# A decoder layer on one core: cross-attention queries projected per tile of 125 rows, low halves moved to GpSimd, and a rearranged prologue

## The reference, cut to what matters

```
x = x + attn(layernorm(x))               # causal, 16 query heads, 4 key/value heads of 128,
                                         # layernorm and rotary embedding of q and k
x = x + cross(layernorm(x), context)     # 32 heads of 16; q, k, v = x Wq.T, ctx Wk.T, ctx Wv.T
                                         # q = q * rsqrt(mean(q*q) + eps) per head, k the same
                                         # softmax(q k.T / 4) v, no output projection
x = x + ffn(layernorm(x))                # 2048 wide, silu(x Wu.T) * (x Wg.T) Wd.T,
                                         # weights rounded to -s, 0, +s with s = mean |W|
```

## Time and profile before

| what | value |
|---|---|
| three executions, median | 1393.27 us |
| the profiled execution's own time | 1391.79 us |
| its span | 1389.7 us |
| TensorE matmul, busy | 1314.8 us (95%) |
| VectorE, busy | 784.6 us (56%) |
| ScalarE, busy | 640.9 us (46%) |
| GpSimd, busy | 274.8 us (20%) |
| mean granted clock of TensorE | 0.984 of full speed |
| chain that ended last | 84% TensorE, 6% VectorE, 3% issue, 1% ScalarE |

### The profile page before, as it was taken

One profiled execution on the slowest core, in us unless ns is written; L12 is line 12 of the kernel. 1 busy time (PEld: TensorE's weight loads), 2 busy tenths in 40 slices (PEclk: granted clock), 3 DMA queues, 4 the chain that ended last, 5 costly groups with the idle time before them and its releaser, 6 DMA issues.

```text
span 1389.7 us, 27539 instructions
## 1 busy us (share of the span) xinstructions
PE 1314.8 (95%) x10968; PEld 867.6 (62%) x10968; DVE 784.6 (56%) x1942; ACT 640.9 (46%) x1452; POOL 274.8 (20%) x266
## 2 busy tenths in 40 slices
PE   7689999999999999999999999999999779999996
PEld 6456666666666666566666666666666446565543
DVE  6987776777677775434445434444346784444422
ACT  3243354333333355366666666666667223232321
POOL 0244452434244441111111111111111000000000
PEclk9799999999999999999999999999999999999999
DMA  8400000000000003111111111112203410000000
GB/s 267 161 1 1 1 1 1 1 1 1 1 1 1 1 1 124 47 58 63 46 46 46 46 45 46 45 47 68 66 25 139 159 68 23 0 24 1 23 1 28
DMA packets 23604, 59.99 MB, mean 43 GB/s; under 512 B 1214, under 2 KB 10811, under 8 KB 20405
## 3 DMA queue, kind: packets, MB, share of 16 engines
q1 hardware_dynamic: 23477, 58.24, 12.6%
HBM read 54.96 MB, written 3.28 MB: 42 GB/s over the span
## 4 chain that ended last, share of the span: by engine, by line
PE 84%; DVE 6%; issue 3%; ACT 1%; DVEq 0%; ACTq 0%
PE A L1616 21%; PE A L1529 11%; PE C L1940 10%; PE A L1583 10%; PE C L1640 6%; PE B L1657 5%; PE C L1569 3%; PE C L1554 3%; PE A L1956 2%; PE B L1956 2%; PE A L1538 2%; PE B L1625 2%; PE B L1562 2%; PE B L1546 2%; DVE qk L1120 1%
## 5 line engine op out<-in xcount | busy, mean ns | idle before, releaser
L1616 PE MATMUL A<-wxhl,arena 128*122 128x512 f16 x1152 | 265.3, 380 | 0.0
L1616 PEld LDWEIGHTS A<-wxhl,arena 128*122 128x122 f16 x1152 | 149.1, 134 | 88.0 <-issue 8.3
L1940 PE MATMUL C<-arena 128*128 128x375 f16 (+1 forms) x1024 | 188.2, 337 | 5.1 <-DVE arena L1121 5.1
L1529 PE MATMUL A<-arena,wxhl 128*125 128x512 f16 (+1 forms) x780 | 174.9, 382 | 6.1 <-DVE tub L960 4.3
L1940 PEld LDWEIGHTS C<-arena 128*128 128x128 bf16 x1024 | 100.4, 98 | 82.7 <-issue 9.6
L506 POOL TENSOR_TENSOR arena<-arena,region 100x512 f32<-100x512 f32 (+1 forms) x64 | 65.9, 1062 | 421.2 <-DVE region L1084 421.2
L690 ACT ACTIVATE arena<-C 122x1600 f32<-122x1600 f32 x96 | 144.3, 1503 | 4.4 <-PE C L1640 2.8
L1529 PEld LDWEIGHTS A<-arena,wxhl 128*125 128x125 f16 (+1 forms) x780 | 105.0, 137 | 65.7 <-DVE tub L960 4.8
L482 POOL TENSOR_TENSOR region<-tub 125x512 f32<-125x512 f32 (+1 forms) x65 | 82.6, 1270 | 265.4 <-DVE tub L960 265.3
L618 ACT ACTIVATE region<-C,negm 100x100 f32<-100x100 f32 x256 | 84.3, 358 | 102.2 <-DVE negm L1004 102.2
L1583 PE MATMUL A<-arena,stageb 128*125 128x512 f16 (+1 forms) x416 | 123.8, 379 | 0.7 <-ACT arena L674 0.7
(11 more groups left out here) (163 smaller groups left out, 2096.5 us busy)
## 6 DMA issues: line engine op xcount, KB each, us to landing
stageb<-in_wffn SPq DMA_DIRECT2D x16, 768.0 KB, 4.7
arena<-in_ctxt SPq DMA_DIRECT2D x16, 722.0 KB, 4.7
stageb<-in_wffn SPq DMA_DIRECT2D x6, 1024.0 KB, 4.8
wxhl<-in_wffn SPq DMA_DIRECT2D x6, 1024.0 KB, 4.8
arena<-in_wqkv SPq DMA_DIRECT2D x4, 1024.0 KB, 15.4
arena<-in_wx SPq DMA_DIRECT2D x3, 1024.0 KB, 6.9
out_x<-xres SPq DMA_DIRECT2D x12, 250.0 KB
xres<-in_x SPq DMA_DIRECT2D x1, 2250.0 KB
```

The source lines that it names most:

```text
L1529: ins = pe.matmul(A[j % 2][0:m, :], xp[:, k, at:at + m], wp[:, j, k, :], start=(n == 0), stop=(n == 11))
L1616: ins = pe.matmul(A[(par + n) % 2][0:rows, :], lhs, wp[:, 0 if n == 0 else 1 if n < 4 else 2, k, :], start=(i == 0), stop=(i == 11))
L1940: ins = pe.matmul(C[2 * (e % 2) + half][:, 0:cols], wf[:, 3 * (e // 4) + half, k, (e % 4) * 128:(e % 4 + 1) * 128], part[:, k, 0:cols], st ...
```

## The change

It has five parts.

1. **Queries per tile.** `project_q(i)` projects the queries of tile i (125 rows), 13 times, in place of 16 `project2(b, 0)`; it is issued at the end of `turn(b)` if `x2_tile(b)` is a tile, which it isn't in turns 2, 7, 12, 14 and 15. `turn_queries(i)` turns all four blocks of the tile at once into B[0], and VectorE's `queries_back(i)` writes them with their parity copies into one of two buffers `qms`. `turn_heads` and `keys_back` only handle keys. At the end of a turn, TensorE's order is now `scores2(b, 5)`, `turn_queries`, `project2(b + 1, 6)`, a wait for `queries_back`, `turn_heads(b + 1, 0)`, `attend2(b, 2)`, `scores2(b + 1, 0)`, and the rest as before.
2. **Low halves of unit 0 on GpSimd.** In unit 0 of the feed-forward part the 16 `hidden_lo` are GpSimd's.
3. **Filler matmuls.** 14 float32 matmuls of 128 columns ahead of the first `centre`, and 14 behind `values_of(0)`.
4. **Output weights.** The low halves of matrices 5, 6, 8 and 7 are made by GpSimd (2048 elements per partition each), after ScalarE has scaled the float32 source in place (`w_scaled`). The waits on them move with them. `w_lo(9)` stays on VectorE and moves from behind the second to behind the fourth group of turn 0. The rotary tables of tiles 1 to 3 are made in the loop of tile 0, not after it.
5. **Head sums.** For tile 0, groups 1 and 3 are scaled by ScalarE (`z_part`, 4 instructions each), not by GpSimd.

The diff, cut to its core:

```
+WARM, FILL = 14, 14
+def q_tile(b):
+    return last_tile(b) if b == 0 or last_tile(b) > last_tile(b - 1) else None
...
 # GpSimd
-            for j in range(5):
+            def w_lo(j, nth):
+                dst, hi = (wql[:, j], wqh[:, j]) if j < 6 else (wohl[:, W_GROUP[j], 1], wohl[:, W_GROUP[j], 0])
+                pool.wait_ge(a_ws, nth)
+                pool.tensor_tensor(dst..., staged(j)[0]..., hi..., ALU.subtract).then_inc(g_wlo, 1)
+            for j in range(3):
                 w_of(0, j)
-            for j in range(5):
-                z_of(0, j)
+            w_lo(5, 1)
+            for j in range(3, 5):
+                w_of(0, j)
+            for j in (0, 2, 4):
+                z_of(0, j, 2 if j else 1)
+            w_lo(6, 2)
+            w_lo(8, 3)
+            w_lo(7, 4)
...
+            n = unit_cols(0)
+            for e in range(ET):
+                pool.wait_ge(*count("a_hh", 0, e + 1))
+                if e >= 2:
+                    pool.wait_ge(*count("pe_dn", 0, e - 1))
+                pool.tensor_tensor(hl[e % 2][:, 0:n], hd[e % 2][:, 0:n], hh[e % 2][:, 0:n], ALU.subtract)\
+                    .then_inc(g_hl, 1)
...
 # ScalarE
                 elif 8 <= j < 10:
-                    act.wait_ge(d_wlo, {8: 1, 9: 4}[j])
+                    act.wait_ge(g_wlo, {8: 1, 9: 3}[j])
...
+            def w_scaled(j):
+                act.activation(staged(j)[0], staged(j)[0], ACT.Copy, scale=SW).then_inc(a_ws, 1)
...
-                if j == 2:
+                if j == 1:
                     w_hi(5)
+                elif j == 2:
+                    w_scaled(5)
+                elif j == 3:
+                    w_hi(6)
+                elif j == 4:
+                    w_scaled(6)
             v_of(0)
+            w_hi(8)
+            z_part(1)
+            z_part(3)
             x_hi(1, A[1])
-            for j in range(6, 10):
-                w_hi(j)
+            w_scaled(8)
+            w_hi(7)
+            w_scaled(7)
+            w_hi(9)
...
                 exp2(b, 5)
+                if end < 2:
+                    values(b + 1, 2, odd)
+                    keys_back(b + 1, 0)
                 out_back(b, 2)
-                if end < 2:
-                    keys_back(b + 1, 0)
-                    values(b + 1, 2, odd)
...
 # VectorE
+            def queries_back(i):
+                n = rows_of(i)
+                dve.wait_ge(*count("pe_qT", i, 1))
+                for b, lo, hi, at in pieces(i):
+                    if b > 1:
+                        dve.wait_ge(*count("pe_sc", b - 2, NU))
+                    q = B[0][:, 0:NT * n]...[:, :, at:at + hi - lo].unsqueeze(2).broadcast_to([128, NT, 2, hi - lo])
+                    ins = dve.tensor_tensor(qms[b % 2][:, :, :, lo:hi], q, parity, ALU.mult)
...
-            dve.wait_ge(ld_g, 32)
-            tables(slice(0, 1))
-            dve.wait_ge(d_tab, 4)
             for j in range(5):
                 if j < 4:
                     for half in range(2):
                         w_centred_lo(j + 1, half)
+                if j == 0:
+                    dve.wait_ge(ld_g, 32)
+                    tables(slice(0, 1), ((0, 2), (1, 0)))
+                    dve.wait_ge(d_tab, 4)
                 proj(0, j)
                 if j == 1:
                     columns()
-                if j == 2:
-                    w_lo(5)
+                elif j == 2:
+                    dve.wait_ge(ld_r, 16)
+                    tables(slice(1, 4), ((0, 2),))
                 elif j == 3:
+                    tables(slice(1, 4), ((1, 0),))
                     dve.wait_ge(ld_x1, 16)
                     row_stats(1, ssq[:, 20:21])
             head_norm(0)
             normed(1, rstd[:, 20:21])
-            dve.wait_ge(ld_r, 16)
-            tables(slice(1, 4))
             dve.wait_ge(d_tab, 10)
-            z_back(0, 0, B[0])
+            for j in range(5):
+                z_back(0, j, B[j % 2])
             x_lo(1, A[1])
-            z_back(0, 1, B[1])
-            w_lo(6)
-            z_back(0, 2, B[0])
-            z_back(0, 3, B[1])
-            w_lo(7)
-            z_back(0, 4, B[0])
...
-                if b == 0:
-                    w_lo(8)
...
-                    if b == 0 and g == 1:
+                    if b == 0 and g == 3:
                         w_lo(9)
...
 # TensorE
+            def project_q(i, par):
+                m, at, n = rows_of(i), i % 4 * TW, 0
+                pe.wait_ge(*count("d_x2", i, 1))
+                for xp, wp in ((x2h, wxh), (x2h, wxl), (x2l, wxh)):
+                    for k in range(KT):
+                        ins = pe.matmul(A[par][0:m, :], xp[:, k, at:at + m], wp[:, 0, k, :], start=(n == 0), stop=(n == 11))
+                        n += 1
...
+            pe.wait_ge(d_warm, 1)
+            for _ in range(WARM):
+                pe.matmul(B[0][:, 0:128], vv[:, 0:128], vv[:, 0:128], start=True, stop=True)
             pe.wait_ge(ld_c, 16)
             centre(0, 0)
...
             values_of(0)
+            for _ in range(FILL):
+                pe.matmul(B[1][:, 0:128], ident, ident, start=True, stop=True)
...
                 scores2(b, 5)
-                attend2(b, 2, par)
                 if end < 2:
                     if o2_tile(b) is not None:
                         pe.wait_ge(*count("d_on", o2_tile(b), 1))
+                    if q_tile(b + 1) is not None:
+                        turn_queries(q_tile(b + 1), odd)
+                    project2(b + 1, 6, odd)
+                    if q_tile(b + 1) is not None:
+                        pe.wait_ge(*count("d_qT", q_tile(b + 1), 1))
                     turn_heads(b + 1, 0, odd)
-                    project2(b + 1, 6, odd)
-
+                attend2(b, 2, par)
+                if end < 2:
                     scores2(b + 1, 0)
                 attend2(b, 3, par)
...
                 if end < 2:
                     turn_heads(b + 1, 1, odd)
-                if end < 1:
-                    project2(b + 2, 0, par)
+                if x2_tile(b) is not None:
+                    pe.wait_ge(*count("a_v2", b + 1, 2))
+                    project_q(x2_tile(b), par)
                 if end < 2:
                     pe.wait_ge(*count("a_T", b + 1, 2))
-                    pe.wait_ge(*count("d_T", b + 1, 2))
```

More of the change, by code:

```diff
@@ L622, in p_back @@
             def p_back(b, g, bank):
+                if b == 0 and g == 0:
+                    act.wait_ge(g_wlo, 2)
                 act.wait_ge(*count("pe_pT", b, g + 1))
@@ L628, in a_hi @@
             def a_hi(b, g):
+                if b == 0 and g == 0:
+                    act.wait_ge(g_wlo, 4)
                 act.wait_ge(*count("pe_av", b, g + 1))
@@ L770, in _ @@
             act.wait_ge(*count("pe_zT", TL - 1, 5))
-            keep_raw(0, 0, 0)
+            keep_q(0, 0)
             p_back(b, 2, B[0])
@@ L788, in _ @@
             exp2(0, 0)
-            keep_raw(1, 0, 1)
+            keep_q(1, 1)
             def turn(b, par, end):
@@ L1178, in _, with tables @@
             normed(0, rs1[:, 0:1])
-            def tables(t):
-                for w, g in ((0, 2), (1, 0)):
+            def tables(t, which):
+                for w, g in which:
                     n = t.stop - t.start
@@ L1341, in _ @@
             row_stats2(1)
-            for n in range(2):
-                square_sums(0, n)
+            square_sums_q(0)
+            square_sums(0, 1)
             for g in range(4):
@@ L1352, in _ @@
             ctx_lo(1)
-            queries_back(0, 0)
-            queries_back(0, 1)
+            queries_back(0)
             add_attn(TL - 1, A[0])
             x2_lo(1, B[0])
-            square_sums(1, 0)
+            square_sums_q(1)
             def turn(b, par, end):
@@ L1403, in turn @@
                     ternary(2, 0)
-                if end < 2:
-                    queries_back(b + 1, 0)
+                if end < 2 and q_tile(b + 1) is not None:
+                    queries_back(q_tile(b + 1))
                 if end == 1:
@@ L1412, in turn @@
                     ctx_lo(b + 2)
-                if end < 2:
-                    queries_back(b + 1, 1)
-                if end < 1:
-                    square_sums(b + 2, 0)
+                if x2_tile(b) is not None:
+                    square_sums_q(x2_tile(b))
                 if o2_tile(b) is not None:
@@ L1458, in unit @@
                 for e in range(ET):
-                    hidden_lo(u, e)
+                    if not first:
+                        hidden_lo(u, e)
                     if first:
@@ L1543, in z_turn @@
                 n = rows_of(i)
-                pe.wait_ge(*count("g_z", i, j + 1))
+                if i == 0 and j % 2:
+                    pe.wait_ge(a_z, j // 2 + 1)
+                else:
+                    pe.wait_ge(*count("g_z", i, j + 1))
                 for h in range(4):
@@ L1822, in _ @@
             p_turn(b, 1, B[1])
-            pe.wait_ge(d_wlo, 6)
+            pe.wait_ge(d_wlo, 2)
             pe.wait_ge(*count("d_x1", TL - 2, 1))
```

(5 more changed lines are left out.)

203 lines of the change are left out of this document (119 added, 84 removed).

## The result

The changed kernel took 1377.74 us (median of four executions, 1376.20 to 1380.27), the kernel before 1393.77 us beside it: a ratio of 0.9888, 95% interval 0.9871 to 0.9906, so 16 us faster. Measured again later, beside 19 executions of the kernel before (median 1392.14, 1388.34 to 1396.21), it was 1376.69 us, ratio 0.9887, interval 0.9868 to 0.9905. The forecast was 1388.8 us with a range down to 1379.5: the sign was right, the size was not. A gain of 4.5 us was forecast, 15 to 16 came.

The account below looks back on a forecast made before the run. TensorE was taken to bound the cross-attention and VectorE unit 0, with the prologue's lead changing hands. The terms -1.0 + 1.7 - 1.5 + 0 - 0.3 - 1.8 - 1.6 = -4.5 us gave 1388.8 us, range 1379.5 to 1395.5.

Parts of the forecast that it names:

- -1.8 for the rounds: Unit 0 of the feed-forward part: six rounds of two blocks each get 0.3 us shorter, -1.8 us.
- 2.1 - 1.8 = 0.3: Unit 0, each round: 2.1 us leave VectorE, two GpSimd low halves block ternary work for 1.8, leaving 0.3 us.
- The rival of a GpSimd that works beside VectorE: Unit 0 and prologue: GpSimd doesn't block VectorE, so -20 us in all, 1373 us; chance 0.06.
- The slow clock in unit 0, -1.6: Unit 0, near 1146 us: a shorter TensorE stall keeps the full clock for the next matmuls, -1.6 us.
- Queries, -1.5: Cross-attention, turns 2, 7 and 12: dropping the query projection there gains 0.5 us in each turn, -1.5 us.
- none of it gets shorter: End of turn 7: ScalarE's work ahead of the turned keys keeps its length, so the next step starts only 0.5 us earlier.
- Turns 14 and 15: End of cross-attention: a new 1.1 us wait and 1.4 us earlier scales, together 0, ends -1.4 and +1.5 us.
- The keys at 583 us: Two key turns at 583 us lose VectorE's step in front of ScalarE's: -0.3 us.
- In full: Cross-attention: the dropped query projections save all 7.8 us of TensorE's work; as a rival 1382.5 us, chance 0.13.
- Prologue, -1.0 and +1.7: Prologue: -1.0 us up to group 2 of tile 1, and +1.7 us for moving `w_lo(9)` behind the fourth group.
- the warm start: Start of the kernel: fillers shorten the first centring by 1.7 us, of which 0.9 us arrives.
- The slower rival: Prologue: mutual blocking of VectorE and GpSimd costs +1.5 + 3 us, in all +3.2, 1396.5 us; chance 0.13.

Follow-up runs that it names:

- the prologue's part alone: The kernel before with only the fillers, the four output-weight low halves on GpSimd and the head sums' scaling on ScalarE: 1390.47 us, ratio 0.9986.
- the whole: The kernel before with all parts of the change, run again for a second profile: 1376.69 us, ratio 0.9887.
- Experiment 2: The changed kernel with unit 0's low halves left out (8 of 375 columns made, `down` taking the high half twice): 1367.91 us, ratio 0.9828.
- experiment 3: The kernel before, unchanged, profiled a second time: the matmuls behind unit 0's stall took 3.92 in place of 2.72 us.
- experiment 6: The changed kernel with each of the four output-weight low halves on GpSimd made in four instructions of 512 columns: 1370.35 us, ratio 0.9841.
- the feed-forward part alone: The kernel before with only unit 0's low halves of the gated products moved to GpSimd: 1385.01 us, ratio 0.9945.

## Why the prediction was right in direction and wrong in size

- **Unit 0, the largest miss.** Forecast -1.8 for the rounds. The step that failed is "2.1 - 1.8 = 0.3": it charged each low half on GpSimd with its whole 0.9 us. The low half does take 0.84 to 0.91 us, but the ternary instruction that it stops loses 0.64 or 0.58: the first ends 1.07 us after GpSimd's where it needs 1.28 alone, so 0.2 us of it is over before it has to stand still. That could be read in the earlier trace rows: the multiply lost 0.71 of the 0.91 us that GpSimd had left. Two of these are 1.22, and 2.1 - 1.22 = 0.9; with 0.09 us less between each `hidden` and the next instruction a round gives the measured 1.07 us. Six rounds would be 6.4; between the first `down` and unit 1's rows it was 5.98 (67.34 to 61.36 us, the prologue's part alone against the whole). Experiment 2 shows that the mechanism, VectorE's sum and exclusion, was right. The rival of a GpSimd that works beside VectorE fell, though its time, 1373, was nearer.
- **The slow clock in unit 0, -1.6.** It came (-1.67), but whether for the forecast's reason is not shown: the slow clock is also gone in two kernels where the stall of 3.05 us stayed (experiment 3). As far as is known the term was luck.
- **Queries, -1.5.** Forecast 0.5 us in each of turns 2, 7 and 12, with the wait named rightly. The step that failed is "none of it gets shorter": from the exponential to the keys ScalarE's work did, by 0.43 us, and the wait is 1.36 us where about 2 were forecast. From cross tile 2 to 12 the three turns gave 2.76 us, 0.9 each and not 0.5. (The marks show it as 63.38 to 62.57 us where a projection is gone and 31.90 to 31.54 us in the turn behind it, which has no queries to turn; the other turns take 0.08 us more, for 125 rows in place of 100.) Turns 14 and 15 were taken as 0 with an end at -1.4; the stretch from cross tile 12 to the first `up_gate` gained 0.88: +1.04 for the new wait, and more than that back, with 1.48 us at the ternary weights. The keys at 583 us gave 0.67 where 0.3 was forecast. In all -4.3 where -1.8 was forecast. "In full" (-7.8) fell by the 1.36 us wait.
- **Prologue, -1.0 and +1.7.** Measured -1.7 by the medians of the prologue's part, interval -4.0 to 0, and -0.7 by the mean of the marks. The pieces placed by hand came within 1.3 us: the blocked projection at 44.19 (44.2 forecast), the scaling at 54.55 (54.5), tile 1 at 63.76 (62.5); group 2 at 71.30 and 73.66 (74.5 to 76.4). Mis-sized were `w_lo` (4.07 us for 4.8: 2.0 ns an element at 2048, against 2.2 at 512 in experiment 6) and the warm start, about 0.5 us for 0.9, as the fillers end up to 2 us after the weights have come. The 1.39 us of a table had GpSimd's blocking in it: one of this form takes 0.55 us alone. The +1.7 for `w_lo(9)` was right, measured +2.0 by the marks and +2.1 by the medians. The Trainium skill (GPSIMD Engine Reference, section 3.1 Elementwise — side-by-side cycle accounting) gives 4497 ns for an addition of 2048 float32 elements on GpSimd. The rows here, float32 less float16, have 4070 to 4390 ns, 2 to 10% under it, and the measurement decides.
- **The slower rival** had its mechanism right and its price wrong. VectorE's negations were caught as it said, for 5.7 to 6.6 us in most profiles, but the projection of tile 1 came 3.0 to 3.7 us earlier and paid for it, and unit 0 and the turns brought what it had left out.
- **What the sum was made against.** The profiled execution stood 1.5 us under the median before, which the forecast added, and the one after 2.5 over it. So of the 11.1 us between forecast and median 7.0 lie between the profiled pair (-11.5 us, -4.5 forecast), and 4.0 are where these two executions stood. Neither the sum nor the range allowed for stretches at half clock, some 4 us between two executions of the same code (the second stage took 502.16 us with the prologue's part alone and 506.08 with the feed-forward part alone).

The errors of unit 0 (4.2), the queries (2.5) and the prologue with `w_lo(9)` (1 to 2) all had one sign. Alone they would have stayed within the range, which reached 9.3 us below the forecast; with the 4.0 us of the clock and the medians on the same side they did not.

## What to carry to other kernels

Before you move work off the engine that bounds a stage, split its cost there into the instruction and the wait in front of it. In unit 0 the low half took 0.47 us of VectorE, and beside GpSimd it takes 0.61 back on average: by these numbers the move of the instruction alone lost 0.14 us each time. What paid was the wait of 0.58 us for `hidden_hi`, which VectorE no longer sits out. A low half that stays on VectorE but stands behind the ternary instructions would save that wait too; by an estimate from experiment 2 and the 0.47 us a round would take 7.58 + 2 x 0.47 = 8.5 us, less than the 8.78 of this change. No run here tests it.

A long GpSimd instruction is another matter: any small instruction of VectorE can be held for its whole length, so cut it in pieces as long as the wait that can be borne (0.4 us more on GpSimd for each low half bought 5 us here). When a part of a change measures as nothing, look for two effects inside it: the prologue's part held 7 us of gain that its own blocking and one moved instruction gave away.

## What was not expected of the hardware

- A VectorE instruction held by GpSimd loses 0.1 to 0.2 us less than what GpSimd has left: 0.64 of 0.85 us in unit 0, 0.71 of 0.91 in the earlier trace rows, 3.87 of 4.00 for the table at 37.46 us. The Trainium skill (SBUF — State Buffer, section Who interferes with whom) says that whoever issues first has the shared ports for its whole instruction and that the other fully blocks. An estimate by that would be a loss of 0.85 us in unit 0; the measurement decides.
- After GpSimd's instruction ends, its next one, queued behind it, can take the ports ahead of a second VectorE instruction: two negations of 0.14 us took 2.59 and 4.11 us, 6.61 together.
- The same 3.05 us wait of TensorE is followed by half clock in two profiles, which costs 1.67 us, and by full clock in two others.
